# Two graph layers with a routed expert layer between them: the expert stage worked slot by slot

## The reference, cut to what matters

```python
# layer 0, graph: mean over neighbours of a linear map
x = x + A @ (LN(x) @ W0 + b0) / deg0[:, None]
# layer 0, experts: each row goes to its best 2 of 8 experts
logits = LN(x) @ Wg + bg;  top 2, weights by softmax over the two
h = gelu(xt @ W1[e] + b1[e])            # 256 -> 1024
x = x + sum over the two e of weight * (h @ W2[e] + b2[e])
# layer 1, graph with self loops, both sides scaled by 1/sqrt(degree)
x = x + relu((D^-1/2 (adj + I) D^-1/2 @ LN(x)) @ WL.T + bL)
# layer 1, a rule on LN(x): 16-wide one-hot fields are shifted as bytes, two one-hot fields are added
x = x + LN(x) + one-hot additions
```

## Time and profile before

| | us |
|---|---|
| median of 3 runs | 1076.75 (1076.18 to 1076.94) |
| the profiled execution | 1072.74 |
| its span | 1070.7 |
| TensorE busy in the span | 952.4 (89%) |
| VectorE, ScalarE, GpSimd busy | 559.0, 404.3, 358.6 |
| block 1, expert stage, last block (start) | 0, 349.5, 791.2 |

### The profile page before, as it was taken

How to read it: one execution, slowest core, us unless ns; L and a number is a source line. 1 busy time by engine, 2 the same in 40 slices (tenths; PEclk the granted TensorE clock), 3 DMA queues, 4 the chain that set the end, 5 groups by cost and what they waited for, 6 DMA issues and landing times. The chain is left out here.

```text
span 1070.7 us, 22182 instructions
## 1 busy us (share of the span) xinstructions
PE 952.4 (89%) x6724; PEld 626.4 (59%) x6725; DVE 559.0 (52%) x1643; ACT 404.3 (38%) x826; POOL 358.6 (33%) x417
## 2 busy tenths in 40 slices
PE   4988999999912899999999999999819999999993
PEld 1444545444511798988989898989603454444541
DVE  6734213127598665656666565656436334161654
ACT  4863768676786332323233232323102101010111
POOL 3410000014476254554545454545425320110110
PEclk9999999999965799999999999999959999999997
DMA  9885898899797433232323333332349978876770
GB/s 335 320 294 183 286 327 323 304 352 369 259 296 191 149 51 50 45 55 40 55 44 55 45 50 49 47 53 42 49 149 392 408 261 298 296 238 195 231 261 32
DMA packets 91313, 200.13 MB, mean 187 GB/s; under 512 B 13344, under 2 KB 47136, under 8 KB 91136
## 3 DMA queue, kind: packets, MB, share of 16 engines
q1 hardware_dynamic: 69248, 164.17, 44.0%
q0 software_dynamic: 17840, 31.15, 15.1%
q10 hardware_dynamic: 4176, 4.19, 1.2%
HBM read 176.54 MB, written 22.94 MB: 186 GB/s over the span
## 5 line engine op out<-in xcount | busy, mean ns | idle before, releaser
L945 PE MATMUL bank<-adj_f,feat 128*128 128x512 f16 x1024 | 239.7, 389 | 17.2 <-DMA adj_f<-in_adjT 15.5
L1215 ACT ACTIVATE act_f<-bank,b_sb 128x256 f32<-128x256 f32 x304 | 127.6, 471 | 282.4 <-PE bank L1161 282.4
L1161 PE MATMUL bank<-rT,experts 128*128 128x256 f16 x1824 | 207.9, 275 | 0.9 <-DVE rT L1228 0.9
L1182 PE MATMUL bank<-experts,act_h 128*128 x1824 | 205.3, 273 | 1.5 <-DVE y_f L1260 1.4
L1161 PEld LDWEIGHTS bank<-rT,experts 128*128 x1824 | 179.4, 99 | 23.1 <-issue 1.2
L1182 PEld LDWEIGHTS bank<-experts,act_h 128*128 128x128 f16 x1824 | 176.7, 98 | 21.9 <-issue 2.1
L1079 POOL DMA_INDIRECT x_rows<-y,token x76 | 122.0, 1605 | 193.1 <-DVE y L1267 170.6
L945 PEld LDWEIGHTS bank<-adj_f,feat 128*128 128x128 f16 x1024 | 97.2, 96 | 143.4 <-issue 16.1
L1603 PE MATMUL bank<-adj_g,feat 128*128 128x512 f16 x768 | 178.5, 386 | 1.0 <-POOL feat L1408 1.0
L829 ACT ACTIVATE spent<-adj_f 128x1024 f16<-128x1024 f32 x128 | 135.1, 1055 | 33.2 <-DMA adj_f<-in_adjT 27.9
L1603 PEld LDWEIGHTS bank<-adj_g,feat 128*128 128x128 f16 x768 | 73.6, 96 | 93.9 <-issue 1.5
(11 more groups left out here) (259 smaller groups left out, 907.8 us busy)
## 6 DMA issues: line engine op xcount, KB each, us to landing
adj_f<-in_adjT SPq DMA_DIRECT2D x128, 512.0 KB, 6.7
adj_g<-in_adjT SPq DMA_DIRECT2D x72, 512.0 KB, 6.2
adj_early<-in_adjT SPq DMA_DIRECT2D x24, 512.0 KB, 6.8
adj_g<-in_adjT SPq DMA_DIRECT2D x48, 256.0 KB, 3.3
unit_f<-in_W SPq DMA_DIRECT2D x16, 512.0 KB, 7.6
stage<-in_W SPq DMA_DIRECT2D x12, 512.0 KB, 6.6
x_ring<-in_x POOLq DMA_DIRECT2D x16, 256.0 KB, 7.5
x_rows<-agg SPq DMA_DIRECT2D x4, 1024.0 KB, 8.9
```

The costliest lines, as they stand in the source:

```text
L945: last = pe.matmul(mine(s)[ib * DC + c][:, :], feat0[:, j, h, c * P:(c + 1) * P], adj_0[j % RING][:, ib * HALF_SWEEP:(ib + 1) * HALF_SWEEP ...
L1161: last = pe.matmul(pb[2 + q][:, k * SLOT:(k + 1) * SLOT], w1_part(e * DC + (f // FQ * W2_UNIT0 + c), wh)[:, (f % FQ) * P:(f % FQ + 1) * P] ...
L1182: last = pe.matmul(pb[6 + r][:, 0:D], act_h[i][:, ah, f, r * P:(r + 1) * P], experts[:, ds(e * DC + (W2_UNIT0 + f // UH), 1), wh, (f % UH) ...
L1215: last = a.activation(act_f[q][:, k, :], pb[2 + q][:, k * SLOT:(k + 1) * SLOT], ACT.Gelu, bias=b1_sb[:, ds(e * FC + (2 * q + k), 1)], scal ...
```

## The change

All three blocks end without GpSimd's drain. In the expert stage `rows`, `rT`, `act_h`, `y` and `token` have one buffer each, and the loops run over single slots up to `LAST_SLOT` = (last end - 1) / 256. TensorE mixes the quarters of the two layers and does the next transposes between them; gathers run three slots ahead instead of four; `take_y` is cut in two. The roots and constants of block 3 are computed at the start of the expert stage, and ScalarE runs one square root after its loop. The warming gather of block 1 comes a few waits later, with one iota more.

```diff
-MORE_PAIRS = 2 * MAX_PAIRS
+LAST_SLOT = 2 * MAX_PAIRS
-    AHEAD = 4
+    AHEAD = 3
-    rows = [w(f"rows{i}", [P, SR, ROW], F32) for i in range(2)]
+    rows = w("rows", [P, SR, ROW], F32)
-    with nc.Block() as block:
+    with nc.Block(no_gpsimd_drain=True) as block:
...
 GpSimd, block 2
+            def rows_free(s):
+                pool.wait_ge(sem("rT_ps_ready"), s + 1)
+                pool.wait_ge(sem("gates_taken"), s + 1)
+                pool.sem_inc(sem("waited"), 1)
+            for s in range(2):
+                pool.wait_ge(sem("rows_loaded"), (s + 1) * 16 * SR)
+                rows_free(s)
+                gather(pool, first_tokens, (s + 1) * SR)
+            take_tokens(0)
+            with pool.Fori(0, last) as s:
+                scaled(s)
+                add_rows(0)
+                rows_free(s + 2)
+                gather(pool, token, AHEAD * SR)
+                landed_until(s, 0)
+                add_rows(1)
+                pool.wait_ge(sem("rows_loaded"), (s + 4) * (16 * SR))
+                landed_until(s, 1)
+                pool.sem_inc(sem("y_free"), 1)
+                take_tokens(s + 1)
+            scaled(last)
+            for r in range(SR):
+                add_rows(r)
+                landed_until(last, r)
...
 TensorE, block 2
-            with pe.Fori(0, more) as pr:
-                first_layer(pr * 2 + 1, 1)
-                next_transposes(pr * 2 + 2, 0, pr + 2)
-                second_layer(pr * 2, 0)
-                first_layer(pr * 2 + 2, 0)
-                next_transposes(pr * 2 + 3, 1, pr + 2)
-                second_layer(pr * 2 + 1, 1)
+            def transposes(s):
+                pe.wait_ge(sem("rows_loaded"), (s + 1) * (16 * SR))
+            def second_layer(s, e, q):
+                pe.wait_ge(sem("act_h_ready"), s * FQ + q + 1 + FQ)
...
+                last.then_inc(sem("act_h_used"), 1)
+            def second_layer_may_begin(s, e):
+                pe.wait_ge(sem("y_taken"), s + 1)
+                pe.wait_ge(sem("w2_parts"), e * 2 + 2)
+            transposes(0)
+            e = expert_of(0)
+            pe.wait_ge(sem("rT_ready"), 1)
+            for q in range(FQ):
+                first_layer(0, e, q)
+            transposes(1)
+            with pe.Fori(0, last_slot) as s:
+                e = expert_of(s + 1)
+                e2 = expert_of(s)
+                pe.wait_ge(sem("rT_ready"), s + 2)
+                first_layer(s + 1, e, 0)
+                second_layer_may_begin(s, e2)
+                second_layer(s, e2, 0)
+                first_layer(s + 1, e, 1)
+                second_layer(s, e2, 1)
+                first_layer(s + 1, e, 2)
+                first_layer(s + 1, e, 3)
+                transposes(s + 2)
+                second_layer(s, e2, 2)
+                second_layer(s, e2, 3)
...
 VectorE, block 2
-            with v.Fori(0, more) as pr:
-                for k in range(2):
-                    s = pr * 2 + (k + 1)
-                    split_hidden(s, (k + 1) % 2)
-                    next_rows(s + 1, k)
-                    take_y(s - 1, k)
+            def split_hidden(s, q):
+                v.wait_ge(sem("act_f_ready"), s * FQ + q + 1 + FQ)
+                v.wait_ge(sem("act_h_used"), s * FQ + q + 1)
...
+            def take_y(s):
+                v.wait_ge(sem("act_h_used"), (s + 2) * FQ)
...
+            def scale_y(s):
+                v.wait_ge(sem("y_taken"), s + 2)
+                v.wait_ge(sem("gates_taken"), s + 1)
+                v.wait_ge(sem("y_free"), s + 1)
...
+            count_inputs()
+            next_rows(0)
+            count_roots()
+            for k in range(2):
+                split_late(k)
+            for q in range(FQ - 1):
+                split_hidden(0, q)
+            next_rows(1)
+            split_hidden(0, FQ - 1)
...
+            with v.Fori(0, last_slot) as s:
+                split_hidden(s + 1, 0)
+                split_hidden(s + 1, 1)
+                next_rows(s + 2)
+                split_hidden(s + 1, 2)
+                take_y(s)
+                split_hidden(s + 1, 3)
+                scale_y(s)
+            take_y(last_slot)
+            scale_y(last_slot)
...
 ScalarE, block 2
+            a.wait_ge(sem("cnt_ready"), 1)
+            a.activation(root[:, :], root_in[:, :], ACT.Sqrt).then_inc(sem("cnt_root"), 1)
...
+            a.activation(root_warm[:, :], std[:, 0:1], ACT.Sqrt)
```

More of the change, by code:

```diff
@@ L1147, in expert_of @@
                 return pe.value_load(table[0:1, ds(s, 1)], min_val=0, max_val=E - 1)
[L1149 to L1161, removed]
-                                                 w1_part(e * DC + (f // FQ * W2_UNIT0 + c), wh)[:, (f % FQ) * P:(f % FQ + 1) * P],
-                                                 rT[i][:, xh, c, :], start=(m == 0), stop=(m == 5))
-                                m += 1
-                    last.then_inc(sem("act_ps_ready"), 1)
@@ new lines, in second_layer @@
+            def second_layer(s, e, q):
+                pe.wait_ge(sem("act_h_ready"), s * FQ + q + 1 + FQ)
+                for k in range(2):
+                    f = 2 * q + k
+                    for ah, wh in ((0, 0), (0, 1), (1, 0)):
+                        for r in range(SR):
+                            last = pe.matmul(pb[6 + r][:, 0:D], act_h[:, ah, f, r * P:(r + 1) * P],
+                                             experts[:, ds(e * DC + (W2_UNIT0 + f // UH), 1), wh,
+                                                     (f % UH) * D:(f % UH + 1) * D].rearrange("p a n -> p (a n)"),
+                                             start=(f == 0 and (ah, wh) == (0, 0)), stop=(f == FC - 1 and ah == 1))
+                last.then_inc(sem("act_h_used"), 1)
@@ L1202, in _ @@
+            e2 = expert_of(last_slot)
+            second_layer_may_begin(last_slot, e2)
+            for q in range(FQ):
+                second_layer(last_slot, e2, q)
         @block.scalar
@@ new lines, in _ @@
+            with a.Fori(0, last_slot + 1) as s:
+                e = a.value_load(table[0:1, ds(s, 1)], min_val=0, max_val=E - 1)
+                for q in range(FQ):
+                    a.wait_ge(sem("act_ps_ready"), s * FQ + q + 1)
+                    a.wait_ge(sem("act_h_ready"), s * FQ + q + 1)
+                    for k in range(2):
+                        last = a.activation(act_f[q][:, k, :], pb[2 + q][:, k * SLOT:(k + 1) * SLOT], ACT.Gelu,
+                                            bias=b1_sb[:, ds(e * FC + (2 * q + k), 1)], scale=1.0 / WS)
+                    last.then_inc(sem("act_f_ready"), 1)
```

240 lines of the change are left out of this document (80 added, 160 removed).

## The result

The changed kernel takes 1125.45 us (median, 1124.61 to 1127.95); the kernel before, on the same chip, 1076.47 (1074.08 to 1076.94). The ratio is 1.0472, 95% interval 1.0449 to 1.0494: slower by 4.7%. Forecast were 1137 us and a range of 1112 to 1178. The profiled execution took 1124.61, its span 1122.8.

The account below looks back on a forecast made before the run. TensorE was taken as the bound, without gaps in the expert stage. One slot fewer but 35 stalls of 2.19 us put the last block at 852.8; plus 278.6, 2.0 and 4.0 gave 1137 us, range 1112 to 1178.

Parts of the forecast that it names:

- E: End of TensorE's iteration in the expert stage; rows forecast at E + 10.05, with 7.86 us of work before the transposes.
- The bound: Expert stage: TensorE busy 300.00 of 300 us, so a new order of work can only open gaps.
- One slot less: Expert loop: 37 slots worked instead of 38, 74 scatters instead of 76, a gain of 10.93 us.
- The ring: Expert loop: transposes, two quarters, y, scatter, gathers, landing, transposes; period 13.12 instead of 10.93, stall 2.19 in 35 iterations.
- The other waits: Expert loop: take_y, rT, act_h and two expert-number loads add nothing to the stall; TensorE idles only before the transposes.
- Start of the stage: Expert stage's start: without the drain, transposes 2.8 us earlier, bounds 2.0 to 3.2; first layer 350.1 to 358.3.
- End of the stage: After the last iterations: GpSimd's scatters in series, last block starts at 852.8 instead of 791.2, missing drain of 5.05 included.
- E35: End of TensorE's iteration 35 in the expert loop, forecast at 830.5 us; the last block then starts at 852.8.
- Last block: Block 3: moved roots let statistics start 0.9 us earlier (0 to 1.0), the rest as before; 278.6 us.
- Rival 1, the clock: Expert loop: TensorE's clock falls in the stall, 1.65 us per slot, up to 1195 us; chance 0.17.
- Rival 2, no stall: Expert loop: no stall, period 10.93, time 1061 us; chance 0.07.
- Rival 3: Expert loop: gather lands with its data, scatter issued while VectorE works; stall 1.0 to 1.5, 1096 to 1113 us; chance 0.08.

Follow-up runs that it names:

- e8: The changed kernel with LAST_SLOT raised by one, so 38 slots are worked as before: 1136.19 us, ratio 1.0566.
- e2: The changed kernel with scale_y(s) ahead of split_hidden(s + 1, 3) on VectorE, nothing else: 1096.83 us, ratio 1.0221.
- the pads: An unused GpSimd product put before the gathers of the changed kernel, large (e4, 1230.77 us) or small (e7, 1194.82 us).
- e5: The changed kernel with gathers four slots ahead, behind the second scatter, row numbers from their own tile: 1069.42 us, ratio 0.9941.
- e9: e5 with the second layer a quarter later on TensorE, its expert number's load moved along: 1060.12 us, ratio 0.9887.
- e3: The kernel before, with its three blocks ending without GpSimd's drain and nothing else: 1066.77 us, ratio 0.9934.
- e11: The kernel before without drains, and with the last block's roots and constants made in the expert stage: 1065.61 us, ratio 0.9936.
- e7: The changed kernel with an unused 128x128 GpSimd product that the gathers wait for: 1194.82 us, ratio 1.1111.
- e4: The changed kernel with an unused 128x512 GpSimd product that the gathers wait for: 1230.77 us, ratio 1.1467.
- e1: The changed kernel with GpSimd's gathers ahead of the wait for scaled y and the first scatter: 1140.02 us, ratio 1.0631.
- e6: e5 with the second layer's expert number loaded behind the first quarter instead of at the loop's head: 1070.93 us, ratio 0.9963.

## Why the prediction was right, point by point

| us in the profiled execution | forecast | measured |
|---|---|---|
| E of slot 0 | 371.3 | 372.9 |
| period | 13.12 | 12.80 |
| E of slot 35 | 830.5 | 821.6 |
| last block starts | 852.8 | 844.2 |
| end of the span | 1131.4 | 1122.8 |

- *The bound.* TensorE without a gap before, and a new order that can only open some: right.
- *One slot less.* 74 scatters. A slot more costs 10 to 12 us in the new loop (e8); the 10.93 in the loop before is measured only as its period.
- *The ring.* The path was right link for link: y, scatter, both gathers, landing, transposes. e2 shortened it, the pads lengthened it and e5 took it away, and the time followed. I had it follow from the single `rows` buffer; but with the same single buffer and the gathers in another place the loop runs at 11.3 and 11.0 (e5, e9). Its size was too large by 0.35: forecast E + 10.05, measured E + 9.70. The term that was off is VectorE's. From E to the start of `y` I had 0.48 + 0.80 + 1.20 = 2.48; the trace shows 0.42 + 0.68 + 1.05 = 2.15. I had added durations and small pauses, but an operation of VectorE starts before the one ahead has ended in the trace: the second split operation ran until 414.17 and `y` started at 414.08. That is most of the 0.33; 0.06 of it lies in the first link. GpSimd's start (0.83) and the landing (1.86 for 1.85, at the stage's start as well) were as forecast. The landing was put together from a scatter's wait less 0.83 and a data tail, so that it is right to 0.01 is luck. From E of slot 0 to E of slot 35 it took 448.7 us instead of 459.2, and these 10.5 are most of the 11.5 by which the median missed.
- *The other waits.* The head of the iteration has a gap of its own (0.38 from E to the first quarter, at 412.31), and I had said that TensorE idles nowhere else. Before the transposes it idles for 1.46 from the end of the last quarter, not for 2.19. I had priced two loads at the head as hidden in the stall, and they are: the two gaps, 0.38 + 1.46 = 1.84 per slot, are just the period's excess, and E + 0.38 + 7.86 still ends before the rows land. e5 shows the price of the head with the stall gone: 11.28 against 10.93, 0.35 per slot or some 12 us in all. The profile's idle time there, 3.45 us of 300, shows less, since busy times of matmuls reach beyond the next start.
- *Start of the stage.* 2.73 saved for 2.8. E of slot 0 came 1.6 later than forecast. The gather before it ended 2.0 later (348.30 for 346.30), in a stage that the change hardly touches; in e3, whose block 1 differs only in its end, it ended at 348.20. The first layer took 7.5 us where I had 8.2.
- *End of the stage.* E35 to the last block is 22.6, forecast 22.3. With both drains, 0.7% by e3.
- *Last block.* 278.6 both times. The roots' 0.9 is in the trace (e11) and not in the time.
- *The median.* I put it 4.0 above the profiled execution, as before; here it is 0.8 above: 3.2 less, of which the later start and end gave back 1.9. The 4.0 was the distance of a single execution from a median, and nothing said that it would come again.
- *Rival 1, the clock.* It didn't decide here, but its mechanism is real: gaps of 2.6 to 3.2 us bring it about in a third of the slots (e7), of 2.9 to 3.7 in two thirds (e4). My stall was forecast at 2.19, and no run had gaps between 1.3 and 2.5 in each slot; where it begins stays open. The two gaps in block 1 that I priced it from don't tell either: behind the one of 2.18 the clock stayed at 1.00, so only the one of 2.77 shows it going down and coming back. A slot with the low clock cost 1.9 (e7), where I had 1.65.
- *Rival 2, no stall.* False for this kernel. For a loop without a stall I had 1061, and e9 takes 1060. That they agree so well is partly luck: my sum had a span of 1054.8 with 6.0 on top, and e9 has 1058.0 with 2.1 on top.
- *Rival 3.* Its stall of 1.0 to 1.5 is what the transposes show (1.46), but with the 0.38 at the head the period is longer than that makes it, and neither of its causes is there: the landing took 1.86, and the scatter waited for VectorE.

The Trainium skill (DMA: Bandwidth & Descriptors, Anatomy of one DMA) gave an estimated 2.3 us for a gather where I took 2.82 from the rows; it is 1.03 + 1.86 = 2.89 in the changed kernel, and the measurement decides.

## What to carry to other kernels

Where the loops of several engines wait for each other in a circle, walk the ring: start at the end of one iteration, follow the release through every engine to where the next iteration needs it, and compare with the work that lies between; the difference is lost in each iteration, whatever the engines' shares say. Add from start to start, not durations. Here two gathers issued while a scatter landed cost GpSimd nothing, and the same two ahead of the scatter added 3.03 us to its round (e1), so before an instruction is moved on a queue, count that queue's own round. And ask of each swap what is late now, for one pair of lines was worth 27 to 29 us in one loop and nothing in the next.

## What the runs showed of the hardware that I had not expected

- GpSimd's own round for two scatters, each waited for, and two gathers is 13.36 us if they are in series (e1); with the gathers in a landing wait it fits in e9's period of 10.98, and GpSimd still idles for 1.2 to 2.0 before the first scatter of a slot. A scatter takes 1.6 to issue (2.06 in some slots of e4, e5 and e7) and 2.5 to 3.1 more until the wait for it ends.
- TensorE starts 1.86 us after a gather's issue has ended, in the ring and at the stage's start (1.92 in e3).
- The granted clock: gaps of 1.3 per slot left it at 1.00 for 400 us; gaps of 2.6 to 3.2 put the next matmuls of 9 of 28 slots at 0.50 (e7), gaps of 2.9 to 3.7 those of 17 of 26 (e4), and which of them isn't told by the gap's own length.
- TensorE had a gap of 0.3 to 0.4 us per slot wherever the second layer's expert number was loaded (e5 at the head, e6 behind the first quarter), and almost none (0.04) with this load and the wait for `y_taken` one quarter later (e9). Which of the two makes it isn't settled.
